# Causal attention in a fused two-layer kernel: long query tiles advanced by single head instead of by pair of heads

## The chip, the cores and the metric

The kernel runs on one core of one Trainium2 chip. The metric is the device time of one execution of the whole program, in microseconds.

## The reference, cut to what matters

Input `x` has 4 sequences of 512 tokens with 512 features. Four blocks follow one another: a small cross attention, a transformer layer with latent attention and a mixture of experts, a second cross attention, a second mixture of experts. The change lies in the attention of the second block:

```
kv_d = x @ kv_d_w;  q_d = x @ q_d_w
k = concat(kv_d @ k_u_w, rope(x @ rope_k_w));  q = concat(q_d @ q_u_w, rope(q_d @ rope_q_w));  v = kv_d @ v_u_w
scores = einsum('bqhd,bkhd->bhqk', q, k) / sqrt(32), masked to k <= q
out = einsum('bhqk,bkhd->bqhd', softmax(scores), v) @ o_w
```

There are 16 heads of 32 features, and all of it is float32. The results are needed in full: nothing of the computation is left out by the change.

## The kernel before, in words

`front` runs this attention and everything up to the first routing. A tile is 128 query rows, so a sequence has four query tiles, i = 0 to 3, and because of the causal mask tile i needs (i+1)·128 keys. A **step** is one query tile and two heads. `STEPS` gives 32 steps for each of the 4 sequences: 16 short ones that alternate between tiles 1 and 0 (256 and 128 keys), then 16 long ones that alternate between tiles 3 and 2 (512 and 384 keys). `is_wide(n)` is true for the long ones. Below, a *pair* is two long steps in a row, one of tile 3 and one of tile 2.

A step runs through three engines:

- TensorE computes the scores of each head (`scores`, L1027, with the mask added by L1028) into a PSUM bank. A short step has both heads in one bank, of two that alternate; a long step has a bank for each head, of three that take turns (`bank_of`).
- VectorE takes the negated row maxima (`maxima`, L816), one instruction for each head.
- ScalarE computes the exponentials and their sums (`exponents`, L689) into `prob`.
- TensorE transposes `prob` in blocks of 128 x 128 (`flip_probs`, L1068): 8 blocks for tile 3, 6 for tile 2. The first four blocks (two key blocks of both heads) go to PSUM bank 4 and the others to bank 5.
- VectorE copies bank 4 into `prob_t` (`prob_t_first`, L823), and in long steps ScalarE copies bank 5 (`prob_t_second`, L697).
- TensorE multiplies with the values for two steps at once (`attend`, L1047), once both steps are copied.

After the last steps of a tile, `denominators` (DVE L831, L832) turns the sums into reciprocals spread over 512 columns, TensorE transposes them (in bank 5), and `attended` (L840, L843) copies them and scales the attended values.

The order on each engine is written out by hand: every engine has its own loop over the steps, the queues are in order, and semaphores tie them together. On TensorE the loop body for step n is: scores of step n+2 (in long steps of the first head only), denominators, `attend` of the pair before, the transposes of step n, other work, and in long steps the scores of the second head of step n+2. On VectorE it is: both maxima of step n+1, the copy of bank 4 of step n-1, `attended`, `denominators`, other work. On ScalarE: both exponentials of step n, then the copy of bank 5 of step n-1, other work. The three `between` functions are that other work: they hand out, by step number, the projections of the next sequence (`plain` L1088, `turned` L1094 to L1096, `rotate` L874 to L881, `queries_flip`, `keys_flip`, `queries_rest`, `keys_rest`, `normed`) and the output projection, second norm and routing of the sequence before. The first sequence has nothing before it and the last nothing after it.

`prob_t` has two buffers, one for each parity of the step.

## Time and profile before

| | us |
|---|---|
| median of 3 runs | 2032.91 (2032.46 to 2034.27) |
| the profiled execution, its own time | 2038.68 |
| its span, first to last instruction | 2036.5 |
| busy in the span: TensorE, VectorE, ScalarE, GpSimd | 1606.6, 1354.6, 1017.8, 884.9 |
| mean granted TensorE clock | 0.869 of full speed |

The attention steps run from about 151 to 656 us of the span; the rest is the input stage before them and the two mixtures of experts after them. Each engine is busy only part of that stretch. The page's summary adds up stages with different limits, so what matters for the change is what each engine waits for inside this stretch.

### The profile page before, as it was taken

Reading aid. Unit: us, or ns where it says so; the run is one execution under the profiler, and the core shown is the slowest. Engines: PE = TensorE matmul, PEld = TensorE weight load, DVE = VectorE, ACT = ScalarE, POOL = GpSimd, SP = SyncE. Lnnn points to the kernel's source line nnn. Section 1 sums busy time; section 2 is a strip of 40 time slices with the busy share of each in tenths; the row PEclk is TensorE's granted clock in tenths of the full one; section 3 lists DMA queues with packets and bytes.
Section 4 is the critical chain, followed back from the end, with each engine's and each line's share of the span. In section 5 each row is a group of like instructions: output and inputs, shape, how many; then the busy total and the mean of one; then the engine's idle time right before and its main releaser. Section 6 shows DMA issues by size and latency. Waiting matters only on the chain. (4 is left out here: it accounts for less than half of the span.)

```text
span 2036.5 us, 33507 instructions
## 1 busy us (share of the span) xinstructions
PE 1606.6 (79%) x8846; PEld 1224.0 (60%) x8847; DVE 1354.6 (67%) x2659; ACT 1017.8 (50%) x1941; POOL 884.9 (43%) x654
## 2 busy tenths in 40 slices
PE   4568697797776669999947652199999999999991
PEld 3445565565455447777726441188888888878881
DVE  7645665565564456667656432189999999999992
ACT  1124534434343046666511100178888888888880
POOL 4100010110201222444413556557887888788881
PEclk8589998898888779999965555599999999999996
DMA  9144234242240253675562113268888888898778
GB/s 324 39 103 105 65 107 99 63 134 53 63 125 1 92 154 101 159 164 102 83 200 76 42 35 94 59 145 178 177 194 183 180 174 201 192 225 202 127 125 278
DMA packets 170842, 266.19 MB, mean 131 GB/s; under 512 B 21856, under 2 KB 97504, under 8 KB 169024
## 3 DMA queue, kind: packets, MB, share of 16 engines
q0 software_dynamic: 52624, 113.84, 28.8%
q1 hardware_dynamic: 118128, 151.24, 25.0%
q8 instruction: 45, 0.74, 0.2%
q14 instruction: 45, 0.37, 0.1%
HBM read 150.55 MB, written 87.33 MB: 117 GB/s over the span
## 5 line engine op out<-in xcount | busy, mean ns | idle before, releaser
L1544 DVE TENSOR_TENSOR moe_w_lo<-moe_w_up,moe_w_hi 128x1536 fp32r<-128x1536 f32 (+1 forms) x216 | 408.3, 1890 | 31.7 <-ACT moe_w_hi L1430 22.1
L1430 ACT ACTIVATE moe_w_hi<-moe_w_up 128x1536 fp32r (+3 forms) x216 | 343.1, 1589 | 20.5 <-SPq L1332 20.5
L1371 POOL DMA_INDIRECT moe_rows<-moe_rows,moe_ids x200 | 317.4, 1587 | 68.2 <-issue 56.4
L1639 PE MATMUL psum<-moe_w_hi,moe_rows_hi 128*128 128x384 f32 (+1 forms) x864 | 323.1, 374 | 18.4 <-DVE moe_rows_lo L1538 18.3
L1640 PE MATMUL psum<-moe_w_lo,moe_rows_hi 128*128 128x384 f32 (+1 forms) x864 | 304.1, 352 | 0.0
L1641 PE MATMUL psum<-moe_w_hi,moe_rows_lo 128*128 128x384 f32 (+1 forms) x864 | 303.7, 352 | 0.0
L1665 PE MATMUL psum<-moe_w_down,moe_hid_t 128*128 (+1 forms) x544 | 268.6, 592 | 1.8 <-DVE moe_tail_t L1532 1.2
L1387 POOL DMA_INDIRECT moe_sum<-moe_res,moe_ids x100 | 163.8, 1638 | 104.8 <-ACT moe_res L1467 54.6
L816 DVE TENSOR_REDUCE neg_top<-psum 128x1 f32<-128x128 f32 (+3 forms) x256 | 118.2, 484 | 126.1 <-PE psum L1028 125.9
L1387 POOL DMA_INDIRECT moe_other<-moe_res,moe_ids x100 | 162.6, 1626 | 88.2 <-ACT moe_res L1467 35.0
L1538 DVE TENSOR_TENSOR moe_rows_lo<-psum,moe_rows_hi 128x512 fp32r<-128x512 f32 x216 | 148.7, 689 | 54.8 <-issue 42.9
L1639 PEld LDWEIGHTS psum<-moe_w_hi,moe_rows_hi 128*128 128x128 f32 x864 | 164.2, 190 | 26.4 <-DVE moe_rows_lo L1538 18.7
L1641 PEld LDWEIGHTS psum<-moe_w_hi,moe_rows_lo 128*128 128x128 f32 x864 | 163.5, 189 | 9.4
L1640 PEld LDWEIGHTS psum<-moe_w_lo,moe_rows_hi 128*128 128x128 f32 x864 | 164.6, 190 | 7.4
L689 ACT ACTIVATE prob<-psum,neg_top 128x128 f32<-128x128 f32 (+3 forms) x256 | 132.4, 527 | 68.1 <-DVE neg_top L816 66.8
L288 POOL DMA_INDIRECT moe_slots<-entry,slot x128 | 125.9, 984 | 87.6 <-DVE slot L1924 42.3
L1416 ACT ACTIVATE moe_rows_hi<-psum 128x512 fp32r<-128x512 f32 x216 | 130.6, 605 | 49.2 <-PE psum L1620 48.5
L1441 ACT ACTIVATE moe_tail_hi<-moe_w_down 128x512 fp32r (+1 forms) x160 | 101.1, 632 | 87.1 <-issue 84.1
L1068 PE MATMUL psum<-const_sb,prob 128*128 128x128 f32 x640 | 105.2, 299 | 48.8 <-DVE prob_t L823 25.4
L1447 ACT ACTIVATE moe_gate<-psum 128x192 f32<-128x192 f32 (+1 forms) x216 | 73.6, 341 | 139.8 <-PE psum L1641 136.9
L1620 PE MATMUL psum<-const_sb,moe_rows 128*128 128x128 f32 x864 | 132.4, 277 | 12.0 <-DMA moe_rows<-moe_rows,moe_ids 6.1
L1467 ACT ACTIVATE moe_res<-psum,moe_weight 128x512 f32<-128x512 f32 x200 | 136.0, 680 | 11.2 <-PE psum L1665 6.1
(270 smaller groups left out, 2925.1 us busy)
## 6 DMA issues: line engine op xcount, KB each, us to landing
moe_w_up<-in_L_ffn_w_gate SPq DMA_DIRECT2D x32, 384.0 KB
moe_w_up<-in_L_ffn_w_up SPq DMA_DIRECT2D x32, 384.0 KB
q_st<-q_hi SPq DMA_DIRECT2D x64, 128.0 KB, 2.6
k_st<-k_hi SPq DMA_DIRECT2D x64, 128.0 KB, 2.7
k_st<-k_lo SPq DMA_DIRECT2D x64, 128.0 KB, 2.7
q_st<-q_lo SPq DMA_DIRECT2D x64, 128.0 KB, 2.7
moe_w_down<-in_L_ffn_w_down SPq DMA_DIRECT2D x32, 256.0 KB
moe_w_down<-in_L_ffn_w_down SPq DMA_DIRECT2D x64, 128.0 KB
```

The costliest lines, as they stand in the source:

```text
L689: sc.activation(prob[:, u, e, 0:(i + 1) * P], score_at(n, e, (i + 1) * P), ACT.Exp, bias=neg_top[:, u, e:e + 1], accum_out=den[:, i, 2 * h ...
L1371: pool.indirect_dma_start(rows[u][:, :], None, d["rows"], bass.IndirectOffsetOnAxis(ids[:, t:t + 1], 0)).then_inc(gathered[u], 16)
L1387: pool.indirect_dma_start(sums[t % 2], bass.IndirectOffsetOnAxis(ids[:, t:t + 1], 0), res[t % RESULTS][:, :], None, compute_op=ALU.add).th ...
L1430: sc.activation(w_hi[u % SPLITS][:, :], w_up[:, bass.ds(at * DC, DC), :].rearrange("p a n -> p (a n)"), ACT.Copy).then_inc(T["wh"], 1)
L1467: sc.activation(res[u % RESULTS][:, :], ps[:, 5 + i, :], ACT.Copy, scale=of_row).then_inc(T["res"], 1)
L1538: v.tensor_tensor(rows_lo[i][:, :], ps[:, i, :], rows_hi[i][:, :].bitcast(F32), ALU.subtract).then_inc(T["rts"], 1)
L1544: v.tensor_tensor(w_lo[u % SPLITS][:, :], w_up[:, bass.ds(at * DC, DC), :].rearrange("p a n -> p (a n)"), w_hi[u % SPLITS][:, :].bitcast(F ...
L1620: last = tr(ps[:, i, k * P:(k + 1) * P], rows[u][:, k * P:(k + 1) * P], ident)
L1639: mm(ps[:, 2 + i, 0:2 * I], hi, w_h, start=(k == 0), stop=False)
L1640: mm(ps[:, 2 + i, 0:2 * I], hi, w_l, start=False, stop=False)
L1641: last = mm(ps[:, 2 + i, 0:2 * I], lo, w_h, start=False, stop=(k == DC - 1))
L1665: done = mm(ps[:, 5 + i, :], hid_t[i][:, j, :], tile_at(w_down, at * n_fc + j), start=(j == 0), stop=(j == n_fc - 1))
```

## The change

A list `UNITS` takes the place of the steps: a short step is one unit, a long step is two, one for each head. All three engine loops go over units.

- Transposes: a unit of a long step puts all its blocks into one bank, those of the first head into bank 4 and those of the second into bank 5. VectorE copies bank 4 and ScalarE bank 5, each 512 columns for tile 3 and 384 for tile 2 (before: 512 on VectorE, and 512 or 256 on ScalarE).
- The scores of unit u+2 are always issued ahead of the transposes of unit u. `bank_of` is as it was.
- `attend` for two steps comes two units after the last of them, and `prob_t` has three buffers so that the copies need not wait for it.
- The denominators' transposes go to bank 3 (except for the last step of a sequence), and each of their four parts has a unit number of its own (`at_unit`).
- In `between`, the work that stood at steps 17 to 29 stands one step later.
- `mean_w`, a constant of the first stage, is moved into that stage's memory.

```diff
+UNITS = [(n, e) for n in range(BATCH * NS) for e in ((None,) if STEPS[n % NS][0] < 2 else (0, 1))]
+LAST_UNIT = {n: at for at, (n, e) in enumerate(UNITS)}
...
-        prob_t = sb("prob_t", [P, 2, 2 * TPB, P])
+        prob_t = sb("prob_t", [P, 3, 2 * TPB, P])
...
+        at_unit = {"den": {}, "den_flip": {}, "den_out": {}, "scaled": {}}
+        for n in range(ALL):
+            if ends(n):
+                later = (1, 2, 3, 5 if is_wide(n) else 4) if n % 2 == 0 else (1, 2, 3, 3) if is_wide(n) else (2, 3, 4, 4)
+                for name, lag in zip(at_unit, later):
+                    at_unit[name].setdefault(LAST_UNIT[n] + lag, []).append(n)
+        DEN_BANK = lambda n: 5 if n % NS == NS - 1 else 3
...
-            for n in range(ALL):
-                exponents(n)
-                if n >= 1:
-                    if is_wide(n - 1):
-                        prob_t_second(n - 1)
-                    between((n - 1) // NS, (n - 1) % NS)
+            for at in range(len(UNITS) + 1):
+                if at < len(UNITS):
+                    exponents(*UNITS[at])
+                if at >= 1:
+                    n, e = UNITS[at - 1]
+                    if e == 1:
+                        prob_t_second(n)
+                    if e != 0:
+                        between(n // NS, n % NS)
...
+            for at in range(len(UNITS) + 4):
+                if at + 1 < len(UNITS):
+                    maxima(*UNITS[at + 1])
+                if 1 <= at <= len(UNITS) and UNITS[at - 1][1] != 1:
+                    prob_t_first(UNITS[at - 1][0])
+                for n in at_unit["den_out"].get(at, ()):
+                    denominators_out(n)
+                for n in at_unit["scaled"].get(at, ()):
+                    scaled(n)
+                for n in at_unit["den"].get(at, ()):
+                    denominators(n)
...
-            def flip_probs(n):
+            def flip_probs(n, e):
                 i, u = STEPS[n % NS][0], n % 2
-                since(pe, S["pta"], n)
-                if is_wide(n):
-                    take(5, "ptb", (n // NS) * wide_steps(NS) + wide_steps(n % NS + 1))
...
+                bank = 5 if e == 1 else 4
+                pe.wait_ge(S["pexp"], 2 * n + heads_of(n, e)[-1] + 1)
+                if e == 1:
+                    take(5, "ptb", copied_second(n))
+                else:
+                    take(4, "pta", copied_first(n))
+                for e in heads_of(n, e):
+                    for j in range(i + 1):
+                        at = block_of(n, e, j) % TPB * P
+                        last = tr(ps[:, bank, at:at + P], prob[:, u, e, j * P:(j + 1) * P], ident)
...
+            for at in range(len(UNITS) + 4):
+                if at + 2 < len(UNITS):
+                    n, e = UNITS[at + 2]
+                    for e in heads_of(n, e):
+                        scores(n, e)
+                if at >= 2 and at - 2 < len(UNITS):
+                    n, e = UNITS[at - 2]
+                    if n % 2 == 1 and e != 0:
+                        attend(n - 1)
+                for n in at_unit["den_flip"].get(at, ()):
+                    denominators(n)
+                if at < len(UNITS):
+                    n, e = UNITS[at]
+                    flip_probs(n, e)
+                    if e != 0:
+                        between(n // NS, n % NS)
```

Two places show how the instructions move. The first is TensorE near the end of the first sequence's long steps, in a pair with no other work. Semaphore names: `f_pexp` exponentials, `f_pta` and `f_ptb` copies of bank 4 and 5, `f_heavy3` the staged queries and keys. Before, for two steps:

```order
L1047 MATMUL psum<-prob_t,v_sb 32x128 [waits f_ptb,f_pta]
L1047 MATMUL psum<-prob_t,v_sb 32x128 x13
L1068 MATMUL psum<-const_sb,prob 128x128 [waits f_ptb,f_pta,f_pexp]
L1068 MATMUL psum<-const_sb,prob 128x128 x7
L1027 MATMUL psum<-k_st,q_st 128x512 [waits f_pexp,f_heavy3]
L1028 MATMUL psum<-future,ident 128x128
L1027 MATMUL psum<-k_st,q_st 128x384 [waits f_pexp,f_heavy3]
L1028 MATMUL psum<-future,ident 128x128
L1068 MATMUL psum<-const_sb,prob 128x128 [waits f_ptb,f_pta,f_pexp]
L1068 MATMUL psum<-const_sb,prob 128x128 x5
```

After, for the unit of a tile-2 step's second head and the one of a tile-3 step's first head (the row behind the last one here is the transposes of its second head):

```order
L1055 MATMUL psum<-k_st,q_st 128x512 [waits f_pexp,f_heavy3]
L1056 MATMUL psum<-future,ident 128x128
L1097 MATMUL psum<-const_sb,prob 128x128 [waits f_ptb,f_pexp]
L1097 MATMUL psum<-const_sb,prob 128x128 x2
L1055 MATMUL psum<-k_st,q_st 128x384 [waits f_pexp,f_heavy3]
L1056 MATMUL psum<-future,ident 128x128
L1097 MATMUL psum<-const_sb,prob 128x128 [waits f_pta,f_pexp]
L1097 MATMUL psum<-const_sb,prob 128x128 x3
L1055 MATMUL psum<-k_st,q_st 128x384 [waits f_pexp,f_heavy3]
L1056 MATMUL psum<-future,ident 128x128
L1075 MATMUL psum<-prob_t,v_sb 32x128 [waits f_ptb,f_pta]
L1075 MATMUL psum<-prob_t,v_sb 32x128 x13
```

Eight or six transposes that waited for both copies and both exponentials have become groups of four or three that wait for one copy and one exponential, and each group has one head's scores right ahead of it.

The second is VectorE in the middle of the same half, where `normed` (`h`) is the other work. Before, one step and the start of the next:

```order
L816 TENSOR_REDUCE neg_top<-psum 128x1 [waits f_pexp,f_st] x2
L823 COPY prob_t<-psum 128x512 [waits f_pv,f_pt]
L852 TENSOR_SCALAR h<-h,mv,rstd 128x512 [waits f_x_in,f_z]
L853 SCALAR_TENSOR_TENSOR h<-h,rms,ln 128x512 [waits f_dve]
L816 TENSOR_REDUCE neg_top<-psum 128x1 [waits f_pexp,f_st] x2
L823 COPY prob_t<-psum 128x512 [waits f_pv,f_pt]
```

After:

```order
L837 TENSOR_REDUCE neg_top<-psum 128x1 [waits f_pexp,f_st]
L844 COPY prob_t<-psum 128x512 [waits f_pv,f_pt]
L837 TENSOR_REDUCE neg_top<-psum 128x1 [waits f_pexp,f_st]
L877 TENSOR_SCALAR h<-h,mv,rstd 128x512 [waits f_x_in,f_z]
L878 SCALAR_TENSOR_TENSOR h<-h,rms,ln 128x512 [waits f_dve]
L837 TENSOR_REDUCE neg_top<-psum 128x1 [waits f_pexp,f_st]
L844 COPY prob_t<-psum 128x384 [waits f_pv,f_pt]
L837 TENSOR_REDUCE neg_top<-psum 128x1 [waits f_pexp,f_st]
```

The two maxima of a step, which stood together ahead of the copy, now stand apart, and the copy comes after the first of them.

## Rows read from the trace of the kernel before

**Rows 1.** Windows of single-head and other halves (us; busy us, instructions per engine; clock; DMA):
```profile
core 0: us, PE busy (x) PEld busy (x) DVE busy (x) ACT busy (x) POOL busy (x), PEclk, DMA share, GB/s
151.00:200.00 49.00, 42.30 (x298) 30.05 (x297) 26.56 (x65) 23.29 (x82) 0.00 (x0) 0.96 0.47 115
200.00:260.00 60.00, 42.36 (x454) 33.48 (x454) 42.09 (x79) 30.63 (x86) 0.00 (x0) 1.00 0.31 71
...
327.00:400.00 73.00, 52.73 (x481) 41.38 (x480) 46.95 (x114) 30.87 (x87) 7.91 (x8) 0.89 0.26 59
...
467.00:542.00 75.00, 53.62 (x480) 41.58 (x477) 42.18 (x107) 31.07 (x87) 7.79 (x8) 0.88 0.25 57
...
597.00:656.00 59.00, 41.23 (x416) 32.38 (x414) 33.63 (x86) 25.42 (x73) 6.46 (x7) 0.87 0.02 3
```

**Rows 2.** Groups of TensorE instructions by line, 200 to 260 us: busy, mean | idle before:
```profile
L1068 PE MATMUL psum<-const_sb,prob 128*128 128x128 f32 x112 | 15.5, 278 | 9.0 <-DVE prob_t L823 5.0 <-issue 2.2 <-DVE att_t L840 1.7
...
L1047 PE MATMUL psum<-prob_t,v_sb 128*32 128x128 f32 x224 | 8.5, 276 | 6.1 <-DVE prob_t L823 6.1
```

**Rows 3.** Windows of one pair of long steps each, columns as in rows 1:
```profile
242.35:248.95 6.60, 4.59 (x56) 3.65 (x55) 5.32 (x10) 4.04 (x11) 0.00 (x0) 1.00 0.56 130
...
604.83:611.02 6.19, 4.16 (x53) 3.22 (x51) 5.13 (x24) 3.48 (x10) 0.00 (x0) 1.00 0.00 0
```

**Rows 4.** Timeline of that first pair: start, duration, engine, line [idle before]:
```profile
242.35 1.10 PE L1068 MATMUL psum<-const_sb,prob 128*128 128x128 f32 x8
...
243.20 0.47 PE L1027 MATMUL psum<-k_st,q_st 128*128 128x512 f32 x1
...
243.48 0.60 ACT L697 ACTIVATE prob_t<-psum 128x512 f32<-128x512 f32 x1 [1.86 <-PE psum L1068]
...
243.78 0.69 DVE L816 TENSOR_REDUCE neg_top<-psum 128x1 f32<-128x512 f32 x1 [0.64 <-PE psum L1028]
...
244.39 0.68 DVE L823 COPY prob_t<-psum 128x512 f32<-128x512 f32 x1
...
245.17 0.85 PE L1068 MATMUL psum<-const_sb,prob 128*128 128x128 f32 x6 [1.13 <-DVE prob_t L823]
...
246.06 0.38 ACT L697 ACTIVATE prob_t<-psum 128x256 f32<-128x256 f32 x1 [0.64 <-PE psum L1068]
...
246.99 0.57 ACT L689 ACTIVATE prob<-psum,neg_top 128x384 f32<-128x384 f32 x1
...
247.22 0.68 DVE L823 COPY prob_t<-psum 128x512 f32<-128x512 f32 x1
...
247.95 1.07 PE L1047 MATMUL psum<-prob_t,v_sb 128*32 128x128 f32 x28 [0.89 <-DVE prob_t L823]
...
248.95 1.10 PE L1068 MATMUL psum<-const_sb,prob 128*128 128x128 f32 x8
```

**Rows 5.** Timeline of a pair that carries projections of the next sequence:
```profile
208.28 1.09 PE L1068 MATMUL psum<-const_sb,prob 128*128 128x128 f32 x8
...
213.26 0.84 PE L1068 MATMUL psum<-const_sb,prob 128*128 128x128 f32 x6 [1.12 <-issue]
...
215.36 0.67 PE L1088 MATMUL psum<-w_q,q_d 128*128 128x256 f32 x2 [1.25 <-DVE qk L881]
...
217.95 1.07 PE L1047 MATMUL psum<-prob_t,v_sb 128*32 128x128 f32 x28 [0.89 <-DVE prob_t L823]
...
218.95 1.09 PE L1068 MATMUL psum<-const_sb,prob 128*128 128x128 f32 x8
```

**Rows 6.** Timeline, from a maximum to the end of its exponential:
```profile
339.16 0.69 DVE L816 TENSOR_REDUCE neg_top<-psum 128x1 f32<-128x512 f32 x1 [2.06 <-PE psum L1028]
...
339.89 0.69 ACT L689 ACTIVATE prob<-psum,neg_top 128x512 f32<-128x512 f32 x1 [1.91 <-DVE neg_top L816]
...
340.48 0.19 ACT L689 ACTIVATION_READ_ACCUMULATOR prob<-psum,neg_top 128x1 f32 x1
```

**Rows 7.** Window in which the clock was low, columns as in rows 1:
```profile
343.50:349.40 5.90, 5.32 (x42) 3.81 (x42) 3.08 (x12) 1.73 (x5) 0.00 (x0) 0.50 0.01 3
```

More of the change, by code:

```diff
@@ L44 @@
 NS = len(STEPS)
-def wide_steps(s):
-    return sum(i >= 2 for i, _ in STEPS[:s])
+UNITS = [(n, e) for n in range(BATCH * NS) for e in ((None,) if STEPS[n % NS][0] < 2 else (0, 1))]
+LAST_UNIT = {n: at for at, (n, e) in enumerate(UNITS)}
 CONST = {}
@@ L482, in _ @@
             for b in range(BATCH):
-                mm(ps[:, 4 + b, :], m["mean_w"][:, :], ctx_sb[0:KEYS, b, :], start=True, stop=True).then_inc(S["means"], 1)
+                mm(ps[:, 4 + b, :], mean_w[:, :], ctx_sb[0:KEYS, b, :], start=True, stop=True).then_inc(S["means"], 1)
             pe.wait_ge(S["ctxts"], BATCH)
@@ L685, in exponents @@
                 if n >= 2:
-                    act.wait_ge(S["pt"], n - 1)
-                for e in range(2):
+                    act.wait_ge(S["pt"], 2 * (n - 2) + heads_of(n, e)[-1] + 1)
+                for e in heads_of(n, e):
                     act.wait_ge(S["ntop"], 2 * n + (e + 1 if is_wide(n) else 2))
@@ L808, in _, with maxima @@
             own = Steps(dve, S["dve"], 0, m["passed"]["dve"])
-            def maxima(n):
+            def maxima(n, e):
                 u, cols = n % 2, (STEPS[n % NS][0] + 1) * P
-                for e in range(2):
+                for e in heads_of(n, e):
                     dve.wait_ge(S["st"], 2 * n + (e + 1 if is_wide(n) else 2))
@@ L983, in _ @@
                 normed(1, t)
-            maxima(0)
-            for n in range(ALL + 2):
-                if n + 1 < ALL:
-                    maxima(n + 1)
-                if 1 <= n <= ALL:
-                    prob_t_first(n - 1)
-                if n >= 2 and ends(n - 2):
-                    attended(n - 2)
-                if 1 <= n <= ALL:
-                    if ends(n - 1):
-                        denominators(n - 1)
-                    between((n - 1) // NS, (n - 1) % NS)
+            maxima(*UNITS[0])
+            for at in range(len(UNITS) + 4):
[9 more added lines that the diff above has]
+                    denominators(n)
+                if 1 <= at <= len(UNITS) and UNITS[at - 1][1] != 0:
+                    n = UNITS[at - 1][0]
+                    between(n // NS, n % NS)
             for n in range(TPB):
@@ L1179, in between @@
                         values(then, s - 12)
[L1180 to L1181 removed]
                     if s in (18, 20):
+                        plain(then, s // 2 - 7)
+                    if s in (19, 21):
                         turned(then, s // 2 - 7)
[L1184 removed]
+                    if s in (22, 26):
                         queries_flip(then, s // 4 - 3)
[L1186 to L1188 removed]
+                    if s in (24, 28):
+                        keys_flip(then, s // 4 - 4)
+                if done >= 0 and s == 30:
                     ranks(done)
@@ L1203, in _ @@
             keys_flip(0, LAST)
-            for n in range(2):
-                for e in range(2):
+            for n, e in UNITS[0:2]:
+                for e in heads_of(n, e):
                     scores(n, e)
-            for n in range(ALL + 2):
-                more = n + 2 < ALL
-                if more:
-                    scores(n + 2, 0)
-                    if not is_wide(n + 2):
-                        scores(n + 2, 1)
-                if n >= 2 and ends(n - 2):
-                    denominators(n - 2)
-                if n % 2 == 0 and 2 <= n <= ALL:
-                    attend(n - 2)
-                if n < ALL:
-                    pe.wait_ge(S["pexp"], 2 * n + 2)
-                    flip_probs(n)
-                    between(n // NS, n % NS)
-                if more and is_wide(n + 2):
-                    scores(n + 2, 1)
+            for at in range(len(UNITS) + 4):
+                if at + 2 < len(UNITS):
+                    n, e = UNITS[at + 2]
+                    for e in heads_of(n, e):
+                        scores(n, e)
[9 more added lines that the diff above has]
+                    if e != 0:
+                        between(n // NS, n % NS)
             for n in range(TPB):
```

94 lines of the change are left out of this document (47 added, 47 removed).

## The prediction

> **What bounds the kernel now.** I read the windows first, one for each half of a sequence [rows 1]. The four long halves take 60, 73, 75 and 59 us, 267 us in all, and TensorE is busy for 42.4, 52.7, 53.6 and 41.2 us of them. No other engine is busier: VectorE has 42.1, 46.9, 42.2 and 33.6. So in these stretches TensorE stands idle for 17.6, 20.3, 21.4 and 17.8 us, 77 us together, and that is what there is to win. The short half shown is busy for 42.3 of its 49 us and has 6.7 us idle.
>
> The groups by line say what TensorE waits for in the first long half: 9.0 us ahead of the transposes and 6.1 us ahead of the value products, mostly for the copies into `prob_t` [rows 2]. The timeline of one pair shows it in order [rows 4]. The eight transposes start at 242.35. Behind them TensorE issues the second head's scores of the step after next, VectorE takes that maximum at 243.78, and only then comes the copy of bank 4, at 244.39, though ScalarE had been able to empty bank 5 at 243.48. The six transposes need bank 4 back, and start at 245.17 after 1.13 us idle. The value products behind them need both steps copied, and VectorE starts that copy at 247.22: 0.89 us idle. The pair lasts 6.60 us, with TensorE busy for 4.59, VectorE for 5.32 and ScalarE for 4.04 [rows 3]. It is a loop of latencies: transposes, score, maximum, copy, transposes.
>
> In the pairs that carry projections, the score of the second head is queued behind the projection as well, and a third wait of 1.25 us appears for the rotation on VectorE; this pair lasts 10.67 us with 3.26 us idle [rows 5].
>
> **What the change does to that loop.** It removes no instruction of weight and adds none: 14 transposes, 4 scores, 28 products, 4 maxima, 4 exponentials and 4 copies in a pair, as before. The copy of bank 4 now follows a maximum whose score was issued before the transposes, so the copy waits for nothing but the transposes. The exponential, its copy and the transposes of one head run while the other head's stand in the other bank.
>
> TensorE's own work in a pair without other work: 4.16 us busy in the last sequence's [rows 3]. I add 0.4 us for two more places at which transposes wait for a semaphore and start over, 4.56 us. What remains is a chain through ScalarE: the second head's transposes of a step, ScalarE's copy (0.60 us of 512 columns [rows 4]), the next second head's exponential (0.57 us of 384 columns [rows 4], and 0.2 us for its sum [rows 6]), transposes. That is about 1.5 us with the pipes' ends, against 1.2 us of TensorE work between the two groups: 0.3 us more. **Such a pair takes 4.9 us.** The chain of one head, score to transposes, is bounded by rows too: a score of 0.47 us and its mask, a maximum of 0.69 [rows 4], an exponential that starts 0.73 us after the maximum and ends 0.78 us later [rows 6], 2.2 us in all. Two units fit in it, so it asks for 1.1 us a unit, 4.4 a pair, and doesn't bind.
>
> With `normed` and one of `queries_rest` or `keys_rest`, VectorE has 5.32 us of work in a pair [rows 3]; its copy of tile 2 shrinks from 512 to 384 columns (0.68 us [rows 4], by about 0.13, from the 0.12 that a maximum or exponential of 384 saves against 512), 5.2 us. I take **5.35 us for a pair of the first three sequences**; in the third there is no `normed`, but ScalarE's `q_hi` or `k_hi` stands inside the chain above.
>
> **The sum**, against the profiled execution's 2038.68 us. Each long half has eight pairs.
> - Pairs 4 to 7 of the first three sequences, 12 of them: 6.60 to 5.35, **-15.0 us**.
> - Pairs 2 and 3 of these, 6 of them: 3.26 us idle [rows 5] of which I leave 0.75 (the rotation still holds back a maximum), **-15.0 us**.
> - The first pair of each half, 4 of them, 1.5 us each: the same waits, less what the change of tiles costs, **-6.0 us**.
> - The last sequence, 6 pairs, from 6.19 us [rows 3] to 4.9: **-7.7 us**.
> - TensorE's clock: in the last three long halves the granted clock is 0.89, 0.88 and 0.87 [rows 1], where the first has 1.00; within one such stretch it is 0.50, the 1.2 GHz level, for 5.9 us [rows 7]. If every such stretch went, half of 16, 18 and 15 us would come back at most, 24.6 us; at least 0. In the first half the same idle share goes with a full clock, so idleness alone doesn't decide it. I take a quarter, **-6.0 us**.
> - Hand-overs: bank 3 is also the output projection's, the rotation's and the routing's. The denominators of the last short steps wait there for routing's first sum, and at the end of a half `residual` on VectorE now stands ahead of the copy that frees bank 5. Priced at nothing to 6 us over all sequences, **+2.0 us**.
> - Short halves: their steps wait in the old way, since both heads share a bank; value products one step later can fill some of 6.7 us. 0, with -4 as the far end. The third `prob_t` buffer, the moved `mean_w` and the shift of `between` by a step cost no instruction; the staging DMAs keep their lead in steps. **0.**
>
> Together -47.7 us, all in front of the mixtures of experts, whose work starts when `front` ends and doesn't change. That is 1991 us for an execution like the profiled one. It lay 5.8 us above the median, so by the median, 2032.9 less 47.7, **1985 us**.
>
> On the clock there is a rule against my quarter. The Trainium skill, TensorE: Matmul & The Clock Gate, "HAM oscillation", says that gaps between bursts of matmuls throttle the clock again, and that a loop which keeps the engine fed stays at the full one. By that rule all 24.6 us would come back, and the sum would be 1966 us. This case's trace agrees in part: the clock does fall in the halves with waits, and doesn't in the first, which waits as much.
>
> A second one bears on the split itself. The Trainium skill, Perfetto Trace Analysis, "Optimizing Scalar/DVE Operations", says that where ScalarE and VectorE aren't saturated but hold up others, breaking up instructions may let work finish sooner, and also that each instruction has a fixed overhead. Here the count stays the same, so only the first half of it applies; but with VectorE at 5.32 of 6.60 us the pairs with `normed` are near the point where it is saturated.
>
> **The rivals.**
> - **ScalarE and VectorE in series (about 2011 us).** If exponentials wait behind the copy in ScalarE's queue for both heads, and maxima behind the copy in VectorE's, then the head's chain of 2.2 us grows by both copies, 0.6 and 0.68, to 3.5 us over two units, 7.0 us for the four units of a pair; I take 5.9, since tile 2's are shorter and a head passes only one of the two copies. Then 18 plain pairs win 0.5 us (9 us), the 6 with projections 1.5 (9 us), the first pairs 1 (4 us): -22 us. For it: the queues are in order. Against it: each copy is due before the instruction behind it is.
> - **The clock comes back (about 1966 us).** The same sum with the whole 24.6 us. For it: low stretches begin where TensorE idles. Against it: the first half's 1.00.
> - **Slower: the units lose their overlap (about 2065 us).** If a unit's transposes hold up TensorE so that the next maximum isn't ready when it is needed, then only one unit is under way where I count on two, and the chain of 2.2 us is paid for more than the 1.65 us that a unit has now (6.60 / 4). At 1.9 us a unit a pair takes 7.6 us, 1 us more than now, and 32 pairs give +32 us. It decides where fewer than 1.33 units are under way. Against it: in the new order the scores of unit u+2 stand ahead of the transposes of u, and three banks let them run.
> - **No change (about 2033 us).** The three score banks are there before, so if the order of VectorE's queue, not of the units, set the pace, and its 5.2 us plus waits filled 6.6, nothing would come of it. The 1.9 us that VectorE doesn't work in the last sequence's and 1.3 in the others' pairs speak against it.
>
> **How the numbers follow.** Forecast as worked out, 1971 to 1999 us: 0.60. Series, 1999 to 2022: 0.20. Clock, 1950 to 1971: 0.14. Slower: 0.04. No change: 0.02. A measurement of this kernel can tell about 0.2%, 4 us, from no change. All but the last two are faster by more: faster 0.94, same 0.02, slower 0.04. For 8 in 10 the range takes the forecast's case, two thirds of the clock's and over half of the series': 1960 to 2013 us. Removing all idle time and all low clock would give 1931 us, which is no case of its own.
>
> **What would show it.** In the profile after: long halves of about 49, 60, 62 and 48 us; TensorE's idle time ahead of transposes and value products in the first of them down from 15 us to under 6, and named for exponentials rather than for `prob_t` copies; a plain pair of 5.3 us, and of 4.9 in the last sequence; the clock of the last three at 0.90 to 0.95; short halves within 2 us of now; everything behind `front` unchanged in length. A plain pair of 5.9 us with transposes that wait for ScalarE means the series case; a clock of 1.00 the third. The prediction is wrong if plain pairs stay at 6 us or more, or if the short halves or the mixtures move by more than 5 us.

## The result, and the profile after it

On the chip of the profile the changed kernel takes **1951.52 us** (median; 1949.34 to 1954.81) against 2033.59 for the kernel before: ratio 0.9589, 95% interval 0.9558 to 0.9619. The forecast was 1985 us and the lower end of its range 1960: it was faster as forecast, by 82 us instead of 48. The profiled execution took 1949.34 us, with a span of 1947.4 and a mean clock of 0.878.

These windows of the changed kernel answer to [rows 1] and [rows 3]: the first short half, the four long ones and the last short one, each from its first transposes to those of the next; then a plain pair (one that carries no projections), and one of the last sequence. Columns as in [rows 1].

```profile
153.31:195.30 41.99, 39.53 (x280) 28.85 (x280) 24.99 (x63) 21.19 (x74) 0.00 (x0) 0.95 0.51 123
195.30:243.50 48.20, 42.34 (x444) 33.26 (x443) 41.58 (x83) 32.68 (x92) 0.00 (x0) 1.00 0.38 87
306.88:358.17 51.29, 44.54 (x460) 35.19 (x459) 45.37 (x116) 32.68 (x93) 1.82 (x2) 1.00 0.38 87
422.81:473.01 50.20, 44.03 (x460) 35.20 (x459) 40.87 (x108) 32.40 (x93) 1.83 (x2) 1.00 0.37 85
473.01:526.36 53.35, 43.39 (x309) 29.18 (x309) 31.53 (x76) 16.55 (x67) 12.26 (x12) 0.90 0.48 119
526.36:566.62 40.26, 34.81 (x401) 27.03 (x400) 32.91 (x87) 26.84 (x76) 0.32 (x1) 1.00 0.15 29
229.79:234.82 5.03, 4.67 (x57) 3.64 (x55) 5.00 (x10) 4.16 (x13) 0.00 (x0) 1.00 0.77 177
549.10:553.55 4.45, 4.15 (x53) 3.20 (x51) 3.45 (x7) 3.52 (x10) 0.00 (x0) 1.00 0.01 4
```

The first long half has about the TensorE work it had, 42.34 us, in 48 us instead of 60, and every long half is at full clock. (The windows of [rows 1] for the second and third long half run some 4 us past them: from first transposes to first transposes they are 69.1 and 71.2 us before, not 73 and 75, and 51.3 and 50.2 now. So some of the 77 us of idle time that I counted for the long halves lay outside them.) In the plain pair VectorE is busy for 5.00 of 5.03 us, so it sets the pace there. In the last sequence, which has less other work, TensorE is the busiest, with 4.15 of 4.45.

TensorE's groups in the first long half, for [rows 2], with the idle time ahead of them behind the bar:

```profile
L1097 PE MATMUL psum<-const_sb,prob 128*128 128x128 f32 x112 | 18.7, 283 | 4.4 <-ACT prob L707 4.4
...
L1075 PE MATMUL psum<-prob_t,v_sb 128*32 128x128 f32 x208 | 8.1, 276 | 0.5 <-DVE att_t L868 0.5
```

15.1 us ahead of the transposes and products have become 4.9, and 4.4 of what is left waits for exponentials. The timeline of the plain pair, for [rows 4]:

```profile
229.79 0.66 PE L1097 MATMUL psum<-const_sb,prob 128*128 128x128 f32 x4
...
230.48 0.60 ACT L716 ACTIVATE prob_t<-psum 128x512 f32<-128x512 f32 x1 [0.56 <-PE psum L1097]
...
231.02 0.50 PE L1097 MATMUL psum<-const_sb,prob 128*128 128x128 f32 x3
...
231.97 0.55 DVE L844 COPY prob_t<-psum 128x384 f32<-128x384 f32 x1
...
232.15 0.69 ACT L707 ACTIVATE prob<-psum,neg_top 128x512 f32<-128x512 f32 x1
...
232.18 0.55 PE L1097 MATMUL psum<-const_sb,prob 128*128 128x128 f32 x3 [0.35 <-ACT prob L707]
...
232.98 0.66 PE L1097 MATMUL psum<-const_sb,prob 128*128 128x128 f32 x4
...
233.82 1.07 PE L1075 MATMUL psum<-prob_t,v_sb 128*32 128x128 f32 x28
```

One group of transposes is under way in one bank while the other bank is copied. The copy at 231.97 begins 0.95 us after its transposes begin and 0.45 after they end, and nobody waits for it: it is done 0.46 us before the transposes at 232.98 write its bank again, and the products at 233.82 start without idle time. One wait of 0.35 us is left in the pair.

### The profile page after: what moved, and what is told of

Read it like the earlier page. It is cut to its first block and busy times, and to the rows that moved or that the text cites. A ratio compares the mean times of both kernels' runs of the same rounds, so it can differ in the third digit from the quotient of the medians.

```text
span 1947.4 us, 33637 instructions
## 1 busy us (share of the span) xinstructions
PE 1578.6 (81%) x8846; PEld 1207.7 (62%) x8847; DVE 1346.9 (69%) x2659; ACT 1017.5 (52%) x1941; POOL 889.6 (46%) x654
## 5 line engine op out<-in xcount | busy, mean ns | idle before, releaser
L1416 POOL DMA_INDIRECT moe_other<-moe_res,moe_ids x100 | 168.0, 1680 | 90.7 <-ACT moe_res L1496 46.2
L1496 ACT ACTIVATE moe_res<-psum,moe_weight 128x512 f32<-128x512 f32 x200 | 135.8, 679 | 11.5 <-PE psum L1694 6.1
L1589 DVE TENSOR_TENSOR moe_hid<-moe_gate,psum 128x192 f32<-128x192 f32 (+1 forms) x216 | 79.2, 367 | 87.1 <-ACT moe_gate L1476 87.1
```

The source lines that it names most:

```text
L1416: pool.indirect_dma_start(sums[t % 2], bass.IndirectOffsetOnAxis(ids[:, t:t + 1], 0), res[t % RESULTS][:, :], None, compute_op=ALU.add).th ...
L1496: sc.activation(res[u % RESULTS][:, :], ps[:, 5 + i, :], ACT.Copy, scale=of_row).then_inc(T["res"], 1)
```

## The experiments

They ran on other chips, where the kernel before takes 1985.5 to 1988.0 us. So each is given as its ratio to the kernel before on its own chip (95% interval), with its median. "Half" below means a stretch between marks that both kernels have: a long half from ScalarE's first copy of bank 5 to its last, a short half from there to the next first one (the very first short half from VectorE's first copy of bank 4). A clock and a length of one half are those of one profiled execution; medians and ratios are of all.

### The two kernels once more

> The kernel before, unchanged, profiled once more as a control beside the next three. If the gain in the short halves belongs to the change, they take 49, 71, 77 and 64 us here again; if some of it belonged to the chip or the execution (stretches of low clock, stalls of instruction fetch), they differ by several us while the long halves' plain pairs stay at 6.60 us.

> The changed kernel, unchanged, as the other control. Ratio to before 0.959 to 0.968; attention stretch, first copy to last, of 410 to 415 us; long halves at a clock of 1.00.

Before: 0.999 (0.997 to 1.0009), 1984.3 us. Changed: 0.9598 (0.9568 to 0.9629), 1909.24 us. The gain is there too: 75 us. The two expectations held in part: the later short halves of the kernel before are 68.0, 74.2 and 55.8 us here, not 71, 77 and 64, so a part of those lengths belonged to the chip or the execution, and the changed kernel's last long half has a clock of 0.94. The eight halves of the kernel before on this chip, short and long in turn:

```profile
153.85:202.58 48.73, 41.75 (x299) 29.61 (x297) 27.04 (x66) 23.05 (x80) 0.00 (x0) 0.97 0.44 109
202.58:259.14 56.56, 39.19 (x411) 30.83 (x410) 39.46 (x74) 29.51 (x81) 0.00 (x0) 1.00 0.30 70
259.14:327.12 67.98, 62.47 (x423) 41.80 (x423) 41.65 (x98) 26.52 (x90) 6.11 (x5) 1.00 0.49 129
327.12:390.70 63.58, 46.87 (x427) 37.03 (x426) 43.43 (x108) 29.74 (x83) 3.30 (x4) 0.89 0.29 67
390.70:464.91 74.21, 69.51 (x423) 46.40 (x423) 42.47 (x99) 26.62 (x90) 10.73 (x10) 0.89 0.38 100
464.91:527.26 62.35, 45.41 (x427) 36.16 (x426) 38.55 (x100) 29.83 (x82) 3.30 (x4) 0.92 0.29 68
527.26:583.02 55.76, 46.13 (x339) 31.99 (x339) 36.13 (x86) 18.60 (x73) 10.72 (x10) 0.91 0.56 132
583.02:633.10 50.08, 34.63 (x374) 27.02 (x373) 30.39 (x81) 25.02 (x73) 3.31 (x4) 0.93 0.01 3
```

And of the changed kernel:

```profile
153.88:196.57 42.69, 40.23 (x297) 29.06 (x295) 25.92 (x64) 22.53 (x79) 0.00 (x0) 0.97 0.53 124
196.57:241.96 45.39, 39.82 (x416) 31.25 (x415) 39.12 (x78) 30.58 (x84) 0.00 (x0) 1.00 0.35 82
241.96:308.15 66.19, 63.45 (x417) 43.24 (x417) 40.19 (x95) 25.93 (x89) 6.08 (x5) 0.95 0.52 136
308.15:356.63 48.48, 41.99 (x432) 33.18 (x431) 42.89 (x111) 30.59 (x84) 1.18 (x1) 1.00 0.37 86
356.63:419.51 62.88, 60.22 (x417) 41.08 (x417) 40.12 (x95) 25.95 (x90) 13.00 (x12) 1.00 0.50 120
419.51:466.90 47.39, 41.47 (x432) 33.17 (x431) 38.40 (x103) 30.30 (x85) 1.08 (x2) 1.00 0.38 88
466.90:516.99 50.09, 44.35 (x333) 31.39 (x333) 33.65 (x81) 17.98 (x73) 12.95 (x12) 0.90 0.60 141
516.99:557.01 40.02, 34.83 (x380) 27.02 (x379) 32.19 (x85) 26.33 (x74) 1.05 (x2) 0.94 0.07 14
```

The spans differ by 75.0 us. The long halves give 51.3 of it (232.6 to 181.3), the short ones 24.8 (246.7 to 221.9), and the part behind the attention loses 1.1 (1349.4 to 1350.5). I had priced the long ones at -49.7 with their clock, and the short ones at nothing. **The short halves are the miss.** On the first chip, by the same marks, the spans differ by 89.1 us: the long halves give 59.3 (239.4 to 180.1), the short ones 27.3 (259.9 to 232.6), the part behind the attention 4.3, and the part ahead of it loses 1.8.

### One order alone: the copy between the two maxima

The kernel before, whose VectorE copies bank 4 behind the first maximum of a long step instead of behind both. Units, buffers and transposes stay. (`maxima` takes the heads as an argument.)

```diff
-                if n + 1 < ALL:
-                    maxima(n + 1)
-                if 1 <= n <= ALL:
-                    prob_t_first(n - 1)
+                split = n + 1 < ALL and is_wide(n + 1)
+                if n + 1 < ALL:
+                    maxima(n + 1, (0,) if split else (0, 1))
+                if 1 <= n <= ALL:
+                    prob_t_first(n - 1)
+                if split:
+                    maxima(n + 1, (1,))
```

> The kernel before with one change of order: on VectorE, in long steps, the copy of bank 4 stands between the two maxima of the next step instead of behind both. Loop theory (the copy waits for the late score of the second head, and this is what idles TensorE): the wait ahead of the six transposes in a plain pair goes from 1.13 us to under 0.3 and the pair from 6.60 to about 5.8 us; with 28 such pairs 15 to 25 us faster, and more if the clock comes back with it. Unit theory (only the two banks and the single heads take the wait away): pair at 6.5 us or more, time within 5 us of before.

Measured: 0.9752 (0.9714 to 0.979), 1935.99 us, 50 us less, twice what was expected at most. Plain pairs take 5.3 us (4.9 in the last sequence). The timeline of one pair:

```profile
232.34 1.09 PE L1071 MATMUL psum<-const_sb,prob 128*128 128x128 f32 x8
...
233.47 0.69 DVE L823 COPY prob_t<-psum 128x512 f32<-128x512 f32 x1
...
234.08 0.68 DVE L816 TENSOR_REDUCE neg_top<-psum 128x1 f32<-128x512 f32 x1
...
234.26 0.85 PE L1071 MATMUL psum<-const_sb,prob 128*128 128x128 f32 x6 [0.23 <-DVE prob_t L823]
```

A pair with projections, and the window of the whole first long half:

```profile
212.72 0.67 PE L1091 MATMUL psum<-w_q,q_d 128*128 128x256 f32 x2 [1.97 <-DVE qk L881]
...
200.28:250.86 50.58, 42.28 (x411) 32.55 (x410) 39.48 (x74) 29.61 (x81) 0.00 (x0) 0.93 0.33 78
```

The copy starts with the end of the transposes and the six transposes wait 0.23 us, where they waited 1.13 [rows 4]. So the loop that I read there (transposes, late score, maximum, copy, transposes) is the bound of a plain pair, and the order of two instructions on VectorE opens it. The long halves fall to 195.4 us, 37 of the 51 us. The short halves, whose order this kernel leaves alone, give 11.6 (246.7 to 235.1), 7.6 of it in the third, which had a clock of 0.89 before and has 1.00 here. The pairs with projections gain nothing in the first sequence (10.66 us against 10.68): the wait of 1.12 us ahead of the six transposes is gone, and the projection waits 1.97 us for the rotation instead of 1.25. In the changed kernel no wait in this half is over 0.68 us, and these pairs take 8.1 and 7.7.

### The exponential's chain

The changed kernel, but the transposes of a first head wait for the exponentials of both heads.

```diff
-                pe.wait_ge(S["pexp"], 2 * n + heads_of(n, e)[-1] + 1)
+                pe.wait_ge(S["pexp"], 2 * n + 2)
```

> The changed kernel, but the first head's transposes of a long step also wait for the second head's exponential, as both did before. Theory that single heads are worth much by themselves: TensorE idles about 0.8 us more a step, plain pairs at 6 us or more, 25 to 40 us slower than the changed kernel. Theory that the freed copy was the matter and the exponentials run ahead: a pair grows by under 0.5 us, under 15 us.

Measured: 0.9901 (0.9884 to 0.9918), 1969.4 us: 60 us more than the changed kernel. Its plain pairs take 6.9 us and up, at 6.4 in the last sequence, and TensorE's transposes from 200 to 240 us read:

```profile
L1097 PE MATMUL psum<-const_sb,prob 128*128 128x128 f32 x66 | 12.8, 318 | 10.7 <-ACT prob L707 10.7
```

The long halves have clocks of 0.89, 0.85, 0.97 and 0.93, so a part of the 60 us is clock. One wait loses most of the gain: the second head's score now stands ahead of transposes that need its neighbour's exponential, and a loop as long as the old one forms through ScalarE. So the units need waits of a single head.

Next, the changed kernel with the copy of bank 4 moved behind the following unit's maximum:

```diff
-                if 1 <= at <= len(UNITS) and UNITS[at - 1][1] != 1:
-                    prob_t_first(UNITS[at - 1][0])
+                if 1 <= at <= len(UNITS) and UNITS[at - 1][1] is None:
+                    prob_t_first(UNITS[at - 1][0])
+                if 2 <= at <= len(UNITS) + 1 and UNITS[at - 2][1] == 0:
+                    prob_t_first(UNITS[at - 2][0])
```

> The changed kernel, but VectorE copies bank 4 a unit later, behind the maximum of the unit after next. If the place of this copy is what matters in the changed kernel too, the first head's transposes of the next step wait for it: plain pairs at 5.8 us or more, 20 us or more slower than the changed kernel. If single heads give the copy slack (bank 4 is needed only two units later), plain pairs grow by under 0.3 us and the kernel by under 10 us.

Measured: 0.9615 (0.9597 to 0.9633), 1911.01 us; plain pairs 5.2 and 4.8 us instead of 5.0 and 4.5. The copy's place was worth 37 us in the long halves while both heads' transposes shared bank 4. Once each head has a bank it is worth 6 us there (187.7 against 181.3, with three of the four clocks at 0.96 or 0.97) and nothing that the medians show: the copy has slack, as seen above.

### When the value products come

`products_early_short` and `products_early_long`: the changed kernel, with the products one unit after their step instead of two, in short or in long steps. `products_later_long`: four units after, in long steps.

```diff
-                if at >= 2 and at - 2 < len(UNITS):
-                    n, e = UNITS[at - 2]
-                    if n % 2 == 1 and e != 0:
-                        attend(n - 1)
+                for lag in (1, 2):
+                    if at >= lag and at - lag < len(UNITS):
+                        n, e = UNITS[at - lag]
+                        if n % 2 == 1 and e != 0 and lag == (2 if is_wide(n) else 1):
+                            attend(n - 1)
```

> The changed kernel with the value products of the short steps back one unit. Theory that the short halves gained by the later products (they fill waits for ScalarE): each short pair takes 0.4 to 0.5 us more, 4 halves of 7 pairs, 11 to 14 us slower than the changed kernel, all of it in the short halves. Theory that they gained at the hand-overs only: within 3 us of the changed kernel.

> The changed kernel with the value products of the long steps back one unit. They then wait for ScalarE's copy of the unit just before. Theory that this wait is on the path: 0.4 to 0.6 us a pair over 32 pairs, 13 to 19 us slower than the changed kernel. Theory that TensorE has slack there because exponentials set its pace: within 3 us.

> The changed kernel with the long steps' value products four units after the last of their steps instead of two, so that they stand ahead of a second head's transposes, where TensorE waits 0.35 us for ScalarE. If the wait is filled: plain pairs down by 0.3 us, 5 to 9 us faster than the changed kernel. If it moves to the next transposes: within 3 us.

Early in short steps: 0.9674 (0.9638 to 0.9711), 1918.91 us. The first short half goes from 42.7 back to 46.7 us, at one clock; plain pairs stay, and the first pair of each long half grows by 0.7 us. Early in long steps: 0.9674 (0.9634 to 0.9714), 1923.34 us, with plain pairs of 6.1 us in the first two sequences, 5.3 and 4.9 in the others. Later: 0.9666 (0.9646 to 0.9685), 1921.01 us, plain pairs 5.2 and 4.8. Two units is the best of the three, and each other place of the products costs 10 to 14 us. For `products_later_long` both expectations failed: nothing was won, and more than 3 us were lost.

`copy_between_late`: copy_between with the short steps' products one step later and a third buffer. Its edit is the line below, with `n % 3` for `n % 2` in `prob_t`, its copies' waits one pair later, and `mean_w` moved as in the change.

```diff
-                if n % 2 == 0 and 2 <= n <= ALL:
+                if n % 2 == 1 and 3 <= n and not is_wide(n - 3):
+                    attend(n - 3)
...
+                if n % 2 == 0 and 2 <= n <= ALL and is_wide(n - 2):
```

> The kernel before with the copy of bank 4 between the two maxima and, besides, the short steps' value products one step later and three prob_t buffers: everything of the change but single-head units, the split of banks by head and bank 3 for the denominators. If the late products are what shortened the first short half (48.7 to 42.7 us), it is 43 to 44 us here and the kernel 8 to 14 us faster than with the copy alone: ratio to before 0.968 to 0.971. If they need the units to pay, ratio 0.975 as with the copy alone.

Measured: 0.9793 (0.976 to 0.9827), 1944.08 us, slower than copy_between. The first short half fell from 47.5 to 44.1 us, but the first pair of each long half grew from between 7.1 and 8.3 to between 9.4 and 12.0. VectorE's `attended` stands where it stood and now waits for the late products, with maxima queued behind it:

```profile
323.94 0.69 DVE L844 TENSOR_TENSOR att_t<-psum,att_t 128x512 f32<-128x512 f32 x1 [4.25 <-PE psum L1051]
```

In the changed kernel `at_unit` gives this multiplication (`scaled`) a time of its own.

### Denominators in bank 5, other work at the old steps

```diff
-        DEN_BANK = lambda n: 5 if n % NS == NS - 1 else 3
+        DEN_BANK = lambda n: 5
```

> The changed kernel with the denominators' transposes back in bank 5 for all tiles. Hand-over theory (the first short half's last steps lost 2.9 us to bank 5 before): second heads' transposes wait until VectorE has emptied bank 5, 1 to 3 us at each of the eight ends of a half, 8 to 20 us slower than the changed kernel, at the ends of the halves. Rival: the pipelining by units hides it, within 3 us.

Measured: 0.9682 (0.9649 to 0.9715), 1921.85 us. The first short half takes 44.2 us instead of 42.7, at one clock, and the first three long halves 0.8 us more each, all at 1.00: 3.9 us that are shown to be the bank's. The third short half, with 6.9 us more, has a clock of 0.90 where the changed kernel has 1.00, so of the 13 us a part is clock.

> The changed kernel with the projections' and routing's share of the long halves back at steps 17 to 29. If the shift by one step matters (the projection then waits for the rotation on VectorE, 1.25 us in the kernel before), the pairs with projections take 1 to 1.5 us more each, six of them, 6 to 9 us slower than the changed kernel, none in the last long half. If it was only for order, within 3 us.

With every step number in `between` as in the kernel before: 0.9603 (0.9579 to 0.9626), 1911.21 us. The shift by a step does nothing that can be measured.

### TensorE's clock by itself

How much of the gain is the clock? These three are the kernel before with useless bf16 products, written where the step's own value products then start over. They do nothing but occupy TensorE while it would be idle. `useless_long`, shown here, puts 12 and 8 into each long pair but the first. `useless_short` puts 6 and 4 into the short steps, `useless_both` does both.

```diff
+            def useless(n, k):
+                i, hp = STEPS[n % NS]
+                c, g = divmod(2 * hp, GH)
+                for _ in range(k):
+                    mm(ps[g * HD:(g + 1) * HD, 6 + i % 2, c * P:(c + 1) * P], ident16[:, 0:HD], future16[:, :], start=True, stop=True)
...
+                    if is_wide(n - 2) and (n - 2) % PHASE >= 2:
+                        useless(n - 2, 8)
                     attend(n - 2)
                 if n < ALL:
+                    if is_wide(n) and n % PHASE >= 2 and n % 2 == 1:
+                        useless(n, 12)
```

> The kernel before, with useless bf16 products of TensorE in the long steps of every sequence: twelve ahead of the six transposes of a tile-2 step and eight ahead of the value products, where a plain pair has 1.13 and 0.89 us of idle time. They write where the step's own value products start over, so no engine waits for them and nothing else reads them. At some 53 ns each they fill about half of both gaps. Theory A (the clock falls because TensorE stands idle in these gaps, and the changed kernel owes its full clock in the long halves to closing them): the granted clock of long halves 2 to 4, 0.87 to 0.93 in kernels of the old order, goes to 0.97 or more, and with it that of the short halves behind them; plain pairs stay at 6.6 and 6.2 us; the attention stretch gets 8 to 20 us shorter. Theory B (the clock falls for another reason, and came back by chance or with the shorter stretch): clocks stay between 0.87 and 0.93, the time is unchanged within 4 us. Theory C (useless products get in the way): plain pairs grow beyond 6.7 us and the kernel is slower.

> The kernel before, with useless products in the short steps alone: four ahead of the transposes of each step and six ahead of the value products of each pair. Theory A (the later short halves of the kernel before are at 0.89 to 0.93 because of what their own steps leave idle): their clock goes to 0.97 or more, and they get some 3 to 6 us shorter each. Theory B (they are low because the long half ahead of them is): their clock stays at 0.93 or lower, and the useless products, 7 of some 53 ns a step where the gap is smaller, cost 0 to 5 us a half.

> Both of these at once. Theory A: clock of every half at 0.97 or more, and what the clock costs the kernel before comes out as one number: the attention stretch 15 to 25 us shorter, which would be the share of the changed kernel's gain that is the clock's. Theory B: as before within 5 us, and the whole gain of the changed kernel lies in its waits.

Measured: 0.9957 (0.9938 to 0.9977), 1977.9 us; 1.0045 (1.0027 to 1.0064), 1996.08 us; 1.0022 (1.0004 to 1.0041), 1989.89 us. The long halves of `useless_long` and the short half between two of them, from its windows:

```profile
201.39:258.19 56.80, 47.85 (x545) 38.36 (x544) 39.53 (x75) 29.51 (x82) 0.00 (x0) 1.00 0.30 71
...
331.93:390.65 58.72, 49.67 (x561) 40.17 (x560) 43.50 (x108) 29.74 (x82) 2.16 (x2) 1.00 0.29 68
390.65:459.06 68.41, 62.79 (x431) 42.07 (x430) 42.53 (x97) 26.50 (x89) 11.86 (x11) 1.00 0.42 113
459.06:519.40 60.34, 51.31 (x561) 41.58 (x560) 38.74 (x100) 29.83 (x82) 3.41 (x4) 0.97 0.30 69
...
579.04:627.79 48.75, 42.14 (x506) 33.52 (x505) 30.54 (x81) 25.01 (x73) 3.04 (x4) 0.96 0.01 2
```

Plain pairs are at 6.6 and 6.2 us as before, and 134 more products leave the first half at 56.8 us (56.6 before): they lie in idle time. Yet the clock of the last three long halves rises from 0.89, 0.92 and 0.93 to 1.00, 0.97 and 0.96, and they are 4.9, 2.0 and 1.3 us shorter. `useless_both` repeats it (1.00, 0.97, 0.97 and 0.97), while the three profiles of the old order without products in these gaps (before, before_again, `useless_short`) have 0.87 to 0.93 there. Work that does nothing makes the kernel 9 us faster by the median, so the idle gaps do lower the clock in these halves. Theory A holds in kind, but not for what it said of the short halves behind them: the second and the last are at 0.91 and 0.89 (1.00 and 0.91 in before_again), and so the attention stretch of the profiled execution is only 4.2 us shorter.

`useless_short` gives the short halves 1.00, 1.00 and 0.97, but they take 71.1 us where the full clock allows 68.0: too many for their gaps. And the first long half, whose code is that of the kernel before and which is at 1.00 there, has 0.94 and takes 59.2 us. The four long halves together lose more than the short ones, 4.4 against 1.9 us in the profiled executions. With both, the last short half falls to 0.86. Theory A's 15 to 25 us are not there in `useless_both`: its long halves are 6.2 us shorter than in before_again (226.4 against 232.6), its short ones 12.3 longer, so the useless products' own time in the short halves outweighs it.

## Why the prediction missed

**The long halves were right in their waits, as a sum.** With `useless_long` the waits can be read at nearly like clocks. Per long half the changed kernel is 11.2, 10.2, 12.9 and 8.7 us shorter (56.6, in before_again, to 45.4; 58.7 to 48.5; 60.3 to 47.4; 48.75 to 40.0), 43.0 in all. The terms for pairs say 11.5 for each of the first three and 9.2 for the last, 43.7 together. The mechanism behind them, the loop, is what copy_between shows. What remains of the 51.3, 8.3 us, is the clock's, for which I took 6.0.

**Within them the sizes were off and offset each other, which was luck.** Steady plain pairs take 5.0 instead of 5.35, and 4.45 instead of 4.9. For the last sequence I had added 0.4 us for places where the transposes start over, and 0.3 for the chain through ScalarE; its TensorE work is still 4.15 us, and 0.3 is all that stands beside it. On the other side, the pair behind the projections still takes 5.7 in the first sequence, and the first pair 6.6, 7.8, 7.9 and 7.8 (before_again: 8.0, 8.1, 8.1 and 7.1), so its -1.5 came once and the last one even grew. Pairs 2 and 3 were forecast at -2.5 and gave -2.6 and -2.5 in the first sequence. The sum names eight pairs to a half and prices seven. The end of a half, pair 7 and what my marks hold of the unpriced pair 8, gave 0.8, 0.3, 2.1 and 2.1 us, against 1.25 for pair 7 alone. And one reading was wrong: in the last sequence's pair VectorE is idle for 1.06 us (6.19 less 5.13, [rows 3]), not the 1.9 that I set against "no change".

**The step that failed is "Short halves: 0, with -4 as the far end", and with it the +2.0 for hand-overs.** The short halves gave 27.3 us on the first chip, where the forecast was made, and 24.8 on the second. I argued from the order of short steps, which is unchanged, and from one window. That window had 6.7 us of idle time, and I let the late products fill none of it. On the second chip the first short half shrank by 6.0 us at one clock, and its idle time from 7.0 to 2.5; on the first chip by 5.8. (It takes 48.6 to 48.7 us wherever its code is that of the kernel before, so chips can be compared here.) Four kernels share these 6.0 out: the hand-over to the first long step 1.2 (copy_between), the late products 3.4 to 4.0 (copy_between_late, products_early_short), bank 3 for the denominators 1.5 (den_bank5). So the hand-overs, for which I feared a wait in bank 3, gained: before, the transposes waited for `attended` to empty bank 5.

In the later short halves the same comes back beside more work. At full clock one takes 68.0 or 68.4 us before and 62.9 after. Its TensorE groups before, by line:

```profile
L1119 PE MATMUL psum<-w_o,att_t 128*128 128x512 f32 x32 | 14.5, 595 | 1.3 <-DVE h L896 1.3
...
L1068 PE MATMUL psum<-const_sb,prob 128*128 128x128 f32 x56 | 9.5, 283 | 1.7 <-DVE prob_t L823 1.2 <-DVE att_t L840 0.4
...
L1017 PE MATMUL psum<-const_sb,over_den 128*128 128x128 f32 x12 | 1.9, 278 | 0.2 <-ACT v_sb L713 0.2
```

and after:

```profile
L1148 PE MATMUL psum<-w_o,att_t 128*128 128x512 f32 x32 | 14.4, 592 | 0.0
...
L1097 PE MATMUL psum<-const_sb,prob 128*128 128x128 f32 x56 | 9.6, 282 | 0.3 <-DVE prob_t L844 0.3
...
L1045 PE MATMUL psum<-const_sb,over_den 128*128 128x128 f32 x8 | 1.3, 280 | 0.0
```

The waits for `h` (the residual on VectorE, which empties bank 3 for the next output projection), `prob_t` and `att_t` are down by 2.7 us. Some 1 us has only moved across my mark into the long half (four of the denominators' transposes and a score). The steps between the two are copy_between 66.6, copy_between_late 65.2, changed 62.9. The last 2.3 lie in bank 3, where den_bank5 has 0.7 us of the wait for `att_t` back, and in the units with `at_unit`: the 1.3 us for `h` are there in both copy_between kernels and in none with units, den_bank5 and products_early_short among them. The last short half gave 5.7 us at 0.91 and 0.90. The order gave 1.4 of it (54.4 in copy_between), the late products 0.2 (54.2). Most of the rest is the same wait for `h`, here 2.7 us, in copy_between and then in the changed kernel:

```profile
L1122 PE MATMUL psum<-w_o,att_t 128*128 128x512 f32 x32 | 14.5, 595 | 2.7 <-DVE h L896 2.7
...
L1148 PE MATMUL psum<-w_o,att_t 128*128 128x512 f32 x32 | 14.4, 593 | 0.0
```

Whether the units or `at_unit` took it away, no run separates.

**The clock.** I took a quarter, 6.0 us of at most 24.6. In the long halves it was some 8 us on the second chip. In the third short half it was 5.8 more (74.2 at 0.89, 68.4 at 1.00 in `useless_long`), and the second gave 3.3 back (66.2 at 0.95, against 62.9 at 1.00), some 11 of the 75 us in all. The Trainium skill, TensorE: Matmul & The Clock Gate, "HAM oscillation", which I set against my quarter, says that gaps between bursts throttle the clock. The traces agree in direction: with the gaps closed all four long halves have 1.00 on the first chip, and the first three on the second (the last has 0.94). But the page's own case is longer waits, for DMA, and the amount of idle time doesn't set the clock here: the first long half of copy_between, with 8.3 us idle, has 0.93, where that of the kernel before, with 17.4 idle, has 1.00. The 24.6 us that I had joined to it was a bound and not a price; in these runs a long half lost 1.3 to 4.9 us to 0.89 to 0.93. On the first chip the kernel before had 0.87 to 0.89 there, and the long halves gave 59.3 us (239.4 to 180.1 by the same marks), 8 more than on the second. If the waits weigh the same on both, that 8 is clock too, and about 16 us there in all. That is argued and was not tested on that chip.

**What would show it:** idle time under 6 us and named for exponentials held (4.9), and the part behind `front` within 5 us held (-4.3 on the first chip, +1.1 on the second). The clock at 0.90 to 0.95 was too low (1.00), the long halves of 49, 60, 62 and 48 us came at 48.2, 51.3, 50.2 and 40.3 (some 4 us of that for the second and third lie in the windows of [rows 1]), and "short halves within 2 us" was the first to fall.

**The rivals.** Series would have kept plain pairs at 5.9 us: they are at 5.0. The clock's case, 1950 to 1971 us, holds the measured time, and its sign, 1.00 in the long halves, was there. But it had the short halves at nothing, and they gave 27.3 us; that its number fits is in part chance. The slower case, too few units under way, is what `flips_wait_both` comes close to, and even it stays 1% faster than the kernel before. No variant beat the changed kernel; two equal it (copy_unit_later, other_work_old_steps).

## What to carry to other kernels

Write down the loop of latencies that closes over the queues, and look for one instruction that stands behind another it doesn't need. Here one copy placed one maximum earlier was worth 50 of 75 us, clock included, before any new unit or buffer. A stretch that looks nearly full still has idle time of its own: price every stretch that the change's instructions pass, with its waits by name, also where "the order stays". And ask for each bank and each late product what stands behind the instruction that frees it.

## What the runs showed of the hardware

- Useless products in idle gaps raised the granted clock of a long half from 0.89 to 1.00 without making a plain pair longer, and the kernel's median fell by 9 us. It is no remedy to keep: the kernel with such products in its short halves, where the gaps are smaller, is 9 us slower than the kernel before.
- A half with less idle time can have the lower clock. The first long half is idle for 17.4 us, in waits of at most 1.34 us, and at 1.00 in all three profiles of the old order whose steps ahead of it are unchanged (before, before_again, `useless_long` with 8.9 idle). In copy_between it is idle for 8.3 us, with two waits of 1.97 us ahead of the instructions at 212.72 and 223.38, and each time the clock is at 0.50, its 1.2 GHz level, from 0.5 to 1 us after the wait ends:

```profile
214.00:217.00 3.00, 3.00 (x33) 2.08 (x33) 1.25 (x2) 1.61 (x5) 0.00 (x0) 0.50 0.00 0
```

- One profile doesn't fix the clock of a half. The third short half of the changed kernel had 0.97 on the first chip and 1.00 on the second, its last long half 1.00 and 0.94. The last short half was at 0.86 to 0.91 in the kernel before, the changed one, copy_between, `useless_long` and `useless_both`, and at 0.96 in other_work_old_steps, which has the changed kernel's code there.
- The first chip is slower than the four others, by 2.3% for the kernel before (2033.6 against 1985.5 to 1988.0). Between the two profiled executions of it, 35 of 54 us lie behind the attention (1384.6 against 1349.4), and between those of the changed kernel 30 (1380.3 against 1350.5). Why, no run shows.
